# Layer 1 attention: another order on VectorE, the first batch ahead of the loop, low weight parts in the layernorm

## The reference, cut to what matters

```python
ln_out = _ln(hidden_states, ln_w, ln_b)
q = _fp8_linear_pertensor(ln_out, wq, wq_scale, q_in_scale).reshape(b, s, g, hpg, d)
q = _ln(q, qln_w, qln_b)
k = ...   # the same with wk, and _ln
v = ...   # the same with wv, no _ln
core = _gqa(q, k, v).reshape(b, s, nh * d)
qx = ...  # the same with wqx, and _ln
kvx = jnp.einsum('bsi,oi->bso', cond, w_kv_x)
...
xout = _gqa(qx, kx, vx).reshape(b, s, nh * d)
cat = jnp.concatenate([core, xout], axis=-1)
catq = _div_clamp_fp8(cat, proj_smooth)
return jnp.einsum('bsi,oi->bso', catq, wproj) * (proj_in_scale * proj_w_scale)
```

## Time and profile before

| | us |
|---|---|
| median of 3 runs | 2673.7 (2672.37 to 2678.76) |
| the profiled execution, its own time | 2675.16 |
| its span, first to last instruction | 2673.4 |
| busy PE / DVE / ACT / POOL | 2277.1 / 1862.6 / 1348.8 / 1201.7 |

### The profile page before, as it was taken

The page is one execution under the profiler, slowest core; times in us unless marked ns, Lnnn a source line. Parts: engine busy times, 40 slices in busy tenths (PEclk is TensorE's granted clock), DMA queues, the critical chain, the costliest instruction groups (busy, mean ns, idle before and its releaser), DMA issues. The chain is left out here.

```text
span 2673.4 us, 47944 instructions
## 1 busy us (share of the span) xinstructions
PE 2277.1 (85%) x16842; PEld 1948.3 (73%) x16842; DVE 1862.6 (70%) x3807; ACT 1348.8 (50%) x3391; POOL 1201.7 (45%) x1633
## 2 busy tenths in 40 slices
PE   5879993788899968999997699996999994658997
PEld 2368883788888868898987588885888883336775
DVE  5855556698888777878787477775555555975776
ACT  2123332677777757777775233331444442435663
POOL 5800113777888777777776111110344442221112
PEclk9989996799999989999999699997999997767998
DMA  3200001100000011000000300001000000001000
GB/s 129 64 32 1 1 1 55 66 13 15 13 13 17 17 54 31 17 15 15 16 7 1 114 24 25 24 13 54 7 7 7 7 3 1 1 26 35 22 22 33
DMA packets 36925, 68.00 MB, mean 25 GB/s; under 512 B 5713, under 2 KB 25489, under 8 KB 34193
## 3 DMA queue, kind: packets, MB, share of 16 engines
q1 hardware_dynamic: 36688, 64.94, 7.5%
HBM read 58.63 MB, written 6.29 MB: 24 GB/s over the span
## 5 line engine op out<-in xcount | busy, mean ns | idle before, releaser
L1197 PE MATMUL bank<-l_wr,l_xq 128*128 128x128 f32 (+1 forms) x2048 | 280.5, 292 | 19.9 <-POOL l_wxr L1553 9.3
L1197 PEld LDWEIGHTS bank<-l_wr,l_xq 128*128 128x128 f32 x2048 | 257.1, 200 | 21.8 <-issue 15.2
L1315 ACT ACTIVATE xn_T<-bank,l_head_b,l_head_w 128x256 f32<-128x256 f32 x256 | 144.6, 565 | 218.1 <-PE bank L1244 218.1
L1575 POOL TENSOR_TENSOR l_cat<-l_yo,l_eo 128x512 fp32r<-128x512 bf16 x128 | 221.2, 1728 | 57.6 <-DVE l_yo L1398 57.6
L790 PE MATMUL bank<-m_xr,m_wgr 128*128 128x512 f32 x864 | 210.9, 394 | 9.2 <-POOL m_wgr L850 9.2
L1449 DVE TENSOR_REDUCE l_rowsum<-xn_T 128x4 f32<-128x512 f32 x128 | 87.8, 686 | 162.0 <-ACT xn_T L1287 160.4
L1568 POOL TENSOR_TENSOR xn_T<-xn_T,l_rowsum 128x512 f32<-128x512 f32 x128 | 143.1, 1118 | 107.0 <-DVE l_rowsum L1490 107.0
L790 PEld LDWEIGHTS bank<-m_xr,m_wgr 128*128 128x128 f32 x864 | 158.9, 190 | 39.3 <-issue 9.2
L1521 POOL TENSOR_TENSOR l_tiny<-l_tiny,l_minus_half 128x6 f32<-128x6 f32 x128 | 172.3, 1346 | 10.7
L1244 PE MATMUL bank<-ident,l_raw 128*128 128x128 f32 x768 | 113.1, 284 | 73.3 <-DVE l_raw L1455 72.2
L1233 PE MATMUL bank<-l_wpr,l_cat 128*128 128x256 f32 x1024 | 166.1, 305 | 1.9 <-POOL l_cat L1575 1.9
(11 more groups left out here) (323 smaller groups left out, 6339.3 us busy)
## 6 DMA issues: line engine op xcount, KB each, us to landing
l_stage<-in_l_w SPq DMA_DIRECT2D x8, 1024.0 KB, 4.9
m_unsplit<-in_m_w SPq DMA_DIRECT2D x14, 384.0 KB, 3.3
m_wg<-in_m_gu SPq DMA_DIRECT2D x18, 256.0 KB, 2.7
x_norm<-in_ctxT_b SPq DMA_DIRECT2D x32, 128.0 KB, 2.0
l_stage<-in_l_wp SPq DMA_DIRECT2D x4, 1024.0 KB, 4.8
l_saved<-l_xs SPq DMA_DIRECT2D x16, 256.0 KB, 2.0
l_xs<-l_saved SPq DMA_DIRECT2D x16, 256.0 KB, 2.6
l2f_w<-in_l_w SPq DMA_DIRECT2D x3, 1024.0 KB, 7.6
```

Source lines behind the costliest of these rows:

```text
L1197: e.matmul(bank[:, to:to + width], XQ[:, q % 2, v, k, :], WR[:, j, part, k, at:at + width], start=k == 0 and part == 0, stop=k == KT - 1 a ...
L1315: e.activation(tok(QT[:, n % 2, 3 * x:3 * x + 2, :]), ps[:, 0:2 * P], ACT.Identity, bias=head_b[:, 2 * x:2 * x + 1], scale=head_w[:, 2 * x ...
L1575: e.tensor_tensor(tok(CAT[:, n % 2, :, :]), YO[:, n % 2, :], EO[:, :], ALU.subtract).then_inc(s_cat.sem, 1)
```

## The change

On VectorE `norm(s-15)` goes from behind the last rounding part to ahead of `sum_probs(s-17)`. Batch 0's norm, transpose, copies, affine parts and rounding, and the first two context loads, stand ahead of the loop; SP's loop program no longer waits for the layernorm. Batch 2's transpose goes behind the first projection. The low parts of groups 0 and 1 are computed by VectorE inside the two calls of `newton_rstd`, those of groups 2 to 5 by VectorE in the loop; 6 and 7 stay on GpSimd. The tables move.

```diff
-        def newton_rstd(e, var, y, t2, eps, shifted, powered):
+        def newton_rstd(e, var, y, t2, eps, shifted, powered, beside=None):
             e.wait_ge(*dve_own.all())
             e.tensor_scalar(var, var, eps, None, ALU.add).then_inc(shifted[0], 1)
+            if beside:
+                beside(e)
             e.wait_ge(*powered)
...
-            LOADS = (1, 5, 8, 10, 12, 14, 75, 76, 79, 80)
-            means_at = {4: 2, 5: 3, 20: 4, 28: 5, 76: 6, 77: 7}
-            centre_at = {4: 2, 5: 3, 22: 4, 30: 5, 76: 6, 77: 7}
-            high_at = {6: 2, 8: 3, 73: 4, 74: 5, 77: 6, 78: 7}
-            low_at = {0: 0, 4: 1, 7: 2, 9: 3, 74: 4, 75: 5, 78: 6, 79: 7}
-            out_at = {10: 0, 11: 1, 12: 2, 13: 3, 81: 4, 82: 5, 83: 6, 84: 7}
+            LOADS = (0, 1, 14, 15, 19, 21, 75, 76, 79, 80)
+            means_at = {11: 2, 12: 3, 24: 4, 30: 5, 76: 6, 77: 7}
+            centre_at = {11: 2, 12: 3, 26: 4, 32: 5, 77: 6, 78: 7}
+            high_at = {12: 2, 13: 3, 73: 4, 74: 5, 77: 6, 78: 7}
+            low_at = {13: 2, 14: 3, 74: 4, 75: 5}
+            pool_low_at = {78: 6, 79: 7}
+            out_at = {17: 0, 18: 1, 19: 2, 20: 3, 81: 4, 82: 5, 83: 6, 84: 7}
...
-            ends = layernorm(ends, "twice", transposed=False)
+            ends = layernorm(ends, "twice", transposed=False, beside=(first_low, second_low))
...
             def sync(e):
-                begin(e, ends)
+                begin(e, m0_ends)
+                for q in range(2):
+                    e.dma_start(CN[:, q, :, :], A["ctxT_b"][q]).then_inc(s_ctx.of(q), 16)
...
             def tensor(e):
                 begin(e, ends)
+                turn_x(e, 0, 0)
                 for s in range(END):
                     if 0 <= s - 13 < N:
                         project(e, s - 13)
-                    if s % J == 2 and s // J < B:
+                    if s % J == 2 and s // J in TURNS:
                         turn_x(e, s // J, s - 15)
+                    if s == 13:
+                        turn_x(e, 2, 0)
...
             def vector(e):
                 begin(e, ends)
                 e.wait_ge(*s_ready(1))
+                norm_x(e, 0)
+                for part in range(5):
+                    quantise_x(e, 0, part)
...
                     if out:
                         round_out(e, s - 19, 0)
+                    if 0 <= s - 15 < N:
+                        norm(e, s - 15)
...
                     if out:
                         round_out(e, s - 19, 3)
-                    if 0 <= s - 15 < N:
-                        norm(e, s - 15)
                     if 0 <= s - 16 < N:
                         maximum(e, s - 16)
```

More of the change, by code:

```diff
@@ L160, in newton_rstd, with layernorm @@
             return e.tensor_tensor(y, y, t2, ALU.mult)
-        def layernorm(ends, kind="once", transposed=True, counted=True):
+        def layernorm(ends, kind="once", transposed=True, counted=True, beside=(None, None)):
             twice = kind != "once"
@@ L190, in vector @@
                 dve_own.did(e.tensor_copy(var2, var))
-                first = newton_rstd(e, var, rstd[:, :], t2, LN_EPS, shifted(1), powered(1))
+                first = newton_rstd(e, var, rstd[:, :], t2, LN_EPS, shifted(1), powered(1), beside[0])
                 if twice:
@@ L197, in vector @@
                     dve_own.did(e.tensor_tensor(var2, var2, rstd[:, :], ALU.mult))
-                    dve_own.did(newton_rstd(e, var2, y2, t2, LN_EPS if kind == "twice" else 1e-6, shifted(2), powered(2)))
+                    dve_own.did(newton_rstd(e, var2, y2, t2, LN_EPS if kind == "twice" else 1e-6, shifted(2), powered(2),
+                                            beside[1]))
                     e.wait_ge(*dve_own.all())
@@ L1160, in sync @@
                         load_weights(e, i)
-                    if s % J == 0 and 1 <= s // J <= Q:
+                    if s % J == 0 and 3 <= s // J <= Q:
                         q = s // J - 1
-                        if q >= 2:
-                            e.wait_ge(*s_cx(q - 1))
+                        e.wait_ge(*s_cx(q - 1))
                         e.dma_start(CN[:, q % 2, :, :], A["ctxT_b"][q % B]).then_inc(s_ctx.of(q), 16)
@@ L1262, in turn_x @@
                 r.then_inc(s_xtr.sem, 1)
+            TURNS = tuple(b for b in range(1, B) if b != 2)
             def tensor(e):
                 begin(e, ends)
+                turn_x(e, 0, 0)
                 for s in range(END):
@@ L1362, in scalar @@
                 e.wait_ge(*s_ready(1))
+                put_xb(e, 0)
+                affine_here(e, 0, 0)
+                affine_here(e, 0, 1)
+                put_cx_high(e, 0)
+                for v in range(NS):
+                    put_xq(e, 0, v)
                 for s in range(END):
@@ L1368, in scalar @@
                         put_probs(e, s - 18)
-                    if r == 2 and b < B:
+                    if r == 2 and 1 <= b < B:
                         put_xb(e, b)
@@ L1455, in norm, with norm_x @@
                 e.tensor_tensor(heads(n), heads(n), bc(rs, 3, P), ALU.mult).then_inc(s_norm.sem, 1)
+            def norm_x(e, b):
+                if b >= 1:
+                    e.wait_ge(*s_xtr(b))
+                e.tensor_scalar(xn, X[:, b, :], mean[:, b:b + 1], rstd[:, b:b + 1], ALU.subtract, ALU.mult).then_inc(s_xn.sem, 1)
             def maximum(e, n):
@@ L1492, in vector @@
                         round_out(e, s - 19, 2)
-                    if s >= 5 and (s - 5) // J < B:
+                    if s >= 9 and (s - 5) // J < B:
                         quantise_x(e, (s - 5) // J, ((s - 5) % J, 4)[(s - 5) % J == 3])
@@ L1496, in vector @@
                         round_out(e, s - 19, 3)
-                    if 0 <= s - 15 < N:
-                        norm(e, s - 15)
                     if 0 <= s - 16 < N:
                         maximum(e, s - 16)
-                    if s >= 7 and r == 3 and (s - 7) // J < B:
+                    if s >= 11 and r == 3 and (s - 7) // J < B:
                         quantise_x(e, (s - 7) // J, 3)
[L1503 to L1508, removed]
+                    if r == 1 and 1 <= s // J < B:
+                        norm_x(e, s // J)
                     if s in means_at:
@@ L1563, in gpsimd @@
                 begin(e, ends)
+                affine(e, 0, 2)
+                affine(e, 0, 3)
+                put_cx_low(e, 0)
                 for s in range(END):
@@ L1577, in gpsimd @@
                         statistics(e, s - 14)
[L1578 removed]
+                    if r == 3 and 1 <= s // J < B:
                         affine(e, s // J, 2)
[L1580 removed]
+                    if r == 0 and 2 <= s // J <= B:
                         affine(e, s // J - 1, 3)
[L1582 removed]
+                    if r == 1 and 3 <= s // J < Q + 2:
                         put_cx_low(e, s // J - 2)
[L1584 to L1585 removed]
+                    if s in pool_low_at:
+                        fill_low(e, pool_low_at[s])
                     if s in out_at:
```

34 lines of the change are left out of this document (22 added, 12 removed).

## The result

| | us | ratio to before, 95% |
|---|---|---|
| before, median of 4 | 2675.78 (2672.37 to 2678.76) | |
| after, median of 4 | 2718.48 (2710.59 to 2723.91) | 1.0162 [1.0143, 1.0182] |
| after, the profiled execution | 2721.82 (span 2720.0) | |

The change makes the kernel 42.7 us slower (1.6%). The forecast was 2716: 42 more than the 2673.7 that three runs of before had given.

The account below looks back on a forecast made before the run. A round of handovers between GpSimd and VectorE was to replace the old loop through `norm` as the bound. +60 (`norm` order) - 12 (start) - 6 (change of weights) = +42 on the profiled 2675.2: 2717, median 2716 us; range 2680 to 2750.

Parts of the forecast that it names:

- The loop: Attention steps: GpSimd and VectorE take turns through `norm`, `sum_probs`, `prob`, `cat`, `statistics`; 7.37 us a round in the second half.
- What comes on top: Second half, once in four steps each: batch norm statistics 0.33 us, `norm` held by the context's low part 0.55; step 7.59.
- rival C: Attention steps: `cat` stays at 1.80 us because smoothing and sums of squares lie beside it; 2786 us, chance 0.08.
- A: Attention steps: `statistics` is done before VectorE reaches `norm`, so TensorE's 6.76 us sets the step; 2618 us, chance 0.09.
- D: Attention steps: ScalarE's `exponent` is late for `sum_probs` anyway and the old loop stays; 2656 us, chance 0.04.
- B: Whole attention: the round is the bare 7.37 us and the start gives its whole 21; 2674 to 2682 us, chance 0.11.
- floor of 6.76 us a step: Second half: TensorE's own work in a step, taken as 7.02 us less its 0.26 us stall.
- The start: Before the steady steps: `norm(0)` 20 us earlier, near 468; net 12 us gained, bounds 21 and 6.
- The second power: Start, GpSimd: it begins just behind group 1's low part on VectorE and loses some 1.6 us.
- The 60: Cost in us of `norm` ahead of the sums: 24 in the first half, 3 and 33 in later steps.
- The 7 us for the out projection's low parts: Steps 17 to 20: four low parts issued by GpSimd hold the next `norm`, 1.8 us a step.
- The change of weights: Steps between the halves: groups 4 and 5 leave GpSimd for VectorE; 6 us gained, between 12 and 0.

Follow-up runs that it names:

- e4: The changed kernel with the power of `statistics` on GpSimd computed twice from the same input: 2888.21 us, ratio to before 1.0801.
- e3: The changed kernel with GpSimd's `statistics(s-14)` at the head of its step, ahead of `prob` and `cat`, `norm` staying early: 2603.79 us, ratio to before 0.9733.
- e1: The changed kernel with `norm(s-15)` back behind the last rounding part, start and weight tables as changed: 2668.58 us, ratio to before 0.9976.
- e2: The kernel before with only `norm(s-15)` moved ahead of `sum_probs(s-17)`: 2727.94 us, ratio to before 1.0198.
- e7: The changed kernel with the low parts of groups 0 and 1 on GpSimd, ahead of its loop: 2720.55 us, ratio to before 1.0172.

## Why the prediction was right

**The loop, term by term.** Read from the rows of after above: `norm` to `sum_probs` 0.88 (predicted 0.87), to `prob` 1.04 (1.07), to `cat` 1.42 (1.42), `cat` to `statistics` 1.24 (1.24), `statistics` to the next `norm` 2.75 (2.77). The round is 7.33 where 7.37 was forecast. It could be this close because each term was a distance from start to start in the earlier trace rows, and in a basic step the new order put nothing new between them.

**What comes on top.** `norm` behind the context's low part takes 1.47 instead of 0.96: 0.51, once in four steps (forecast 0.55). The batch norm statistics give 0.32 once (0.33): steps of 7.34, 7.84, 7.34 and 7.66. Their mean is 7.55, forecast 7.59. In the first half four steps are 8.19, 8.08, 7.99 and 7.87, 32.1 us together; forecast 32.2.

**The price of `cat`, where rival C parted from the forecast.** 1.15 to 1.17 us in all 128, where the earlier trace rows had 1.81 beside a `norm`. With no `norm` under way when it started, `cat` lost nothing, and smoothing (one input in PSUM) and sums of squares beside it did not stretch it. The rule of the Trainium skill on the shared ports ("SBUF — State Buffer", section "Who interferes with whom") is borne out here.

**Rivals.** A (the loop does not close) falls with 183.8 us of idle time ahead of `norm` and with e4. D (the exponent is late anyway) falls with 6.5 us ahead of `sum_probs`. B gave the loop no additions and the start its whole 21 us; the additions are there, and the start up to `norm(8)` gave 18.1. A's and my own floor of 6.76 us a step was too high: e3 runs at 6.53.

**The start.** First projection forecast 444, measured 445.1; the next two 458 and 464, measured 458.3 and 465.2; `norm(0)` 468, measured 470.8. Most of what was missed is the 2.57 us of the first L1559 (median 0.20): it started at 465.62, just ahead of group 3's low part on VectorE (two instructions, 465.78 to 468.13), and ended with it, at 468.19. The second power lost 1.45 (forecast 1.6).

**Where sizes were off, and hid one another.** The move of `norm` was priced at 60 us and the rest at -18. In medians e1 and e2 give 50 to 52 and -7. By the marks up to the last `cat` it is 50 and -11; the other 4 us of the rest are in the scatter behind it. What was mis-sized:
- The 60 lacked the gain in steps that weights delay: 3.9 us up to (8) and 2.0 in the change of weights. The rest is 2.5 to 3 us less in each half.
- The 7 us for the out projection's low parts in steps 17 to 20 were about twice too much. Like is to be held against like: from (0) to (8) the kernel after takes 64.2 us where e2, with the same early `norm`, takes 60.4, and e1 takes 68.1 where before, with the late one, takes 64.7: 3.8 and 3.4. Of four `norm` behind such a part only one was held, 3.10 us at 496.65. Against that, from (8) to (53) e1 takes 3.0 more than before, which no term had.
- The change of weights was to gain 6. It gained 3.4 in after and 1.4 in e1. The steps with the low parts of groups 4 and 5 came out near the forecast: `norm(59)` to (61) stand 9.6 and 9.1 us apart, where it had 9.0 and before 10.7. That low parts ahead of `norm` hold it was right; VectorE and GpSimd of the kernel after, timeline:
```profile
990.78 3.47 POOL L1123 TENSOR_TENSOR l_wr<-l_stage,l_wr 128x1536 fp32r<-128x1536 f32 x1
990.82 3.51 DVE L1041 TENSOR_SCALAR l_stage<-l_stage,l_means 128x128 f32<-128x128 f32 x1
...
1036.73 2.37 POOL L1591 TENSOR_TENSOR l_wpr<-l_stage,l_wpr 128x1024 fp32r<-128x1024 f32 x1
1036.80 3.11 DVE L1489 TENSOR_TENSOR l_raw<-l_raw,l_tiny 128x768 f32<-128x768 f32 x1 [1.82 <-POOL l_tiny L1569]
```
In the lower pair `norm` starts 0.07 us behind the low part and lasts 3.11 instead of 0.96; these steps are 9.2 to 9.5 us, forecast 9.6. The upper pair is what the forecast missed. With the centring of group 7 moved to step 78, its last instruction (L1041, 0.27 us elsewhere) stands 0.04 us behind GpSimd's low part of group 6 and takes 3.51; ScalarE's high part waits 2.7 us for it. That step, `norm(63)` to (64), takes 13.2 us; forecast was 11.5, and before it took 10.7. The same hold is in e1 and e7 (3.51 in both), and not in before and e2, where the centring stands a step earlier. In e4 the low part comes when the centring is over, and the step takes 12.9 us: the forecast's 11.5 and the 1.40 of the second power.

So the total was right to 2.5 us partly because a cost 10 us too high stood against a gain 11 us too high (7 by the marks). And of the 42.7 only 39 stand in the attention, of which alone the forecast spoke. That much is luck. The sign and the mechanism do not hang on that: the part that decides was measured alone, twice.

## What to carry to other kernels

When two engines hand work to each other once a step, write down the round before reordering one of them: add the distances from start to start along the handovers, in each engine's new order. If the sum is over the present step, the move that removes the visible wait makes the kernel slower, however idle all engines look; the cure is to reorder the partner too (here six small instructions moved on GpSimd turned +1.6% into -2.7%). To test whether such a round is the bound, add one instruction of known length to it: where it is, the instruction costs its whole length a step (1.40 of 1.40 us here), and where it is not, only what is over the time in hand (0.39 of 1.40 in the old order).

## What the runs showed of the hardware that I had not expected

- A power on GpSimd (128x16, 2.93 us from 426.66) and a two-input VectorE instruction of 1,536 elements a partition, started 0.56 us into it, ran side by side: 1.76 us for the one, and the power no longer than undisturbed (2.90 and 2.93 in e7). The other way round, the power started 0.16 us behind the same instruction, and took 4.35. So here a power gives way, and does not hold. The Trainium skill ("SBUF — State Buffer", section "Who interferes with whom") speaks of the pair of ports as held for the whole instruction; for a power that comes first the measurement shows otherwise, and it decides.
- For other GpSimd instructions the holding is as long as that section of the Trainium skill has it: in e7 a VectorE instruction of 0.43 us took 3.52 behind L1123 on GpSimd, and `norm` in e2 up to 4.20 behind a low part of a weight group.
- The smallest instructions are held too. In e3 the six-element L1559 beside `norm` takes 0.99 us instead of 0.20. TensorE has no marked wait there, so that this shows no price.
- The idle time that the brackets show was less than TensorE's slack: 0.26 us shown a step, 0.49 found (7.02 to 6.53), at a granted clock of 1.00 in both.
